# Moving the token normalisation of three cross attentions from VectorE to GpSimd

## The chip, the cores and the metric

The kernel runs on one core of a Trainium2 chip. The metric is the device time of one execution in microseconds (us). The engines have one instruction queue each and run side by side, tied by semaphores: TensorE (PE, matrix products), VectorE (DVE), ScalarE (ACT), GpSimd (POOL) and SyncE (SP, which issues transfers).

## The reference, cut to what matters

Sixteen sequences of 256 tokens, 128 wide, go through four layers of attention and feed-forward. Each attention takes the layer-normed tokens as queries and adds its result to the tokens. Three of the attentions, called `l0`, `l1c` and `l3` in the kernel, are cross attentions onto a context of 64 keys with 16 heads of 8, and each begins with the same norm:

```python
def _layernorm(x, axis=-1, eps=1e-05):
    m = jnp.mean(x, axis=axis, keepdims=True)
    v = jnp.var(x, axis=axis, keepdims=True)
    return (x - m) / jnp.sqrt(v + eps)

x = x + _L0_xattn_ref(_layernorm(x), ctx_512, ctx_512, ...)     # l0
x = x + _L1_xattn_ref(_layernorm(x), ctx_512, ...)              # l1s (self) and l1c (cross)
x = x + _L3_xattn_ref(_layernorm(x), ctx_512, ...)              # l3
```

## The kernel before

The tokens `x` stay in SBUF for the whole program as 32 tiles of 128 tokens, `[128, 32, 128]` in float32, two tiles for each of the 16 sequences. One function, `attention_rows`, builds five attentions. `units` (`U`) is the number of pieces into which the heads of one sequence are cut: `U` is 1 in `l0`, `l1c` and `l3`, where one step of the loop does one whole sequence, and 4 in the self attentions `l1s` and `a1`. The trace leaves digits at the end of a name out, so `l_xn` is the tile `xn` of `l0` (about 22 to 148 us of the span) and of `l3` (about 2296 to 2417 us); `l1c_xn` is that of `l1c` (about 741 to 869 us).

Each engine walks through the same steps j, in a software pipeline that `emit` writes out, and in step j works on different sequences. `at(k)` gives the sequence j + k. With one unit there are 4 steps of lead. In step j, in this order on each queue:

- DVE: `maxima` of sequence j+1, first half (L808); `ln_apply` of j+3 (L792, two instructions, one for each tile, that write `xn`); `ln_stats` of j+4 (L776 and L781: two bn_stats, two bn_aggr into `mv`); `residuals` of j-2 (L877); `maxima` of j+1, second half; then the end of sequence j-1: `turn_sums` (L817), `divide` (L822, L828) and `turn_back` (L838).
- POOL: `context` of j+2 (L967); `lay_values` of j+1 (L993), which first waits for `pv_done`, the value product of sequence j-1; `rstds` of j+4 (L931 and L933: variance plus epsilon, then the power -0.5); `preset` of j+1 where there is an output bias (L961, in `l0` and `l1c`); `keys` of j+2 (L978, two instructions).
- PE: `shift` of j (L533); `turn` of j+2 (L439: `xn` transposed, in both tiles); `scores` of j+1, first half (L485); `values` of j-1 (L566); `project_out` of j-2 (L608, L611); `scores` of j+1, second half; `scores_t` of j+1 (L500); `project_qk` of j+2 (L449, L451, L454), which waits for the residual of j-2, since both use the bank `psum_act`.
- ACT: the two exponentials of j (L668), `turned` of j+2 (L675), `copy_qk` of j+2 (L691, L694, L698), and in `l1c` one copy more (L729).

`turn` of j+2 waits for `proj_out` of j+1, that is for the last of the copies of ACT (L698) in the step before. There is one buffer `xn`, one `mv` and one `rstd`. `ln_apply` of sequence b therefore waits for `xn_turned` to reach b (the transpose of sequence b-1). The statistics of the next sequence come behind `ln_apply` on the same queue, so nothing need guard `mv`.

Of the kernel before, what the change touches and what calls it, by code (L numbers as in the profile page):

```python
# [12 lines left out]
ALU = mybir.AluOpType  # L13
AX = mybir.AxisListType

P = 128
NB = 16
T = 256
TT = T // P
# [16 lines left out]
def wait(eng, sem, value):  # L36

    if isinstance(value, int) and value <= 0:
        return
    eng.wait_ge(sem, value)  # L40
# [234 lines left out]
def attention_rows(nc, name, K, W, *, dh, units, x, out, after=None, norms=(), affine_q=None, affine_kv=None,  # L275
# [10 lines left out]
    U = units  # L286
# [19 lines left out]
    with ExitStack() as ctx:  # L306
        def sb(nm, shape, dt=F32):
            return ctx.enter_context(nc.sbuf_tensor(f"{name}_{nm}", shape, dt))

        def sem(nm):  # L310
            return nc.alloc_semaphore(f"{name}_{nm}")
# [13 lines left out]
        xn = sb("xn", [P, TT, P])  # L325
        mv = sb("mv", [P, NLN, TT, 2])
        st6 = sb("st6", [P, NLN, TT, 6])
        rstd = sb("rstd", [P, NLN, TT])
# [21 lines left out]
        if add_t is not None:  # L350
# [8 lines left out]
        xn_ready, xn_turned = sem("xn_ready"), sem("xn_turned")  # L359
        laid = sem("laid")  # L360
        st_step, stats, veps_ready, rstd_ready, scaled, gained, shifted = (
            [sem(f"{nm}{i}") for i in range(NLN)]
            for nm in ("st_step", "stats", "veps_ready", "rstd_ready", "scaled", "gained", "shifted"))
# [47 lines left out]
        def inside(n, limit=N):  # L411
            return not isinstance(n, int) or 0 <= n < limit

        block = ctx.enter_context(nc.Block())

        @block.sync
# [318 lines left out]
        def _(dve):  # L735
# [31 lines left out]
            def ln_stats(b, i):  # L767
                src = (x if i == 0 else residual)[:, bass.ds(b * TT, TT), :]
                if i > 0:
                    ready = shifted if norms[i - 1] is not None else scaled  # L770
                    dve.wait_ge(ready[i - 1], b + 1)
                elif merge:
                    dve.wait_ge(merged, 2 * TT * (b + 1))
                dve.sem_inc(K["passed"], 1)
                for t in range(TT):
                    last = dve.bn_stats(st6[:, i, t, :], src[:, t, :])  # L776
                last.then_inc(st_step[i], 1)
                dve.wait_ge(st_step[i], b + 1)
                dve.sem_inc(K["passed"], 1)
                for t in range(TT):  # L780
                    last = dve.bn_aggr(mv[:, i, t, :], st6[:, i, t, :])  # L781
                last.then_inc(stats[i], 1)

            def ln_apply(b, i):
                dve.wait_ge(rstd_ready[i], b + 1)
                src = (x if i == 0 else residual)[:, bass.ds(b * TT, TT), :]
                final = i == NLN - 1
                if final:
                    wait(dve, xn_turned, b)
                dst = xn if final else residual[:, bass.ds(b * TT, TT), :]  # L790
                for t in range(TT):
                    last = dve.tensor_scalar(dst[:, t, :], src[:, t, :], mv[:, i, t, 0:1], rstd[:, i, t:t + 1],  # L792
                                             ALU.subtract, ALU.mult)
                last.then_inc(xn_ready if final else scaled[i], 1)

            def maxima(n, pos, half):

                dve.wait_ge(s_ready, 2 * n + half + 1)
                if half == 0:
                    wait(dve, st_ready, 2 * (n - 1))  # L800
                src = psum_s[:, :, 0:SC].rearrange("p i (h k) -> p i h k", k=P if before else NK)
                dst = negm[:, pos % 2, :, 2 * half * CG:2 * (half + 1) * CG]
                if U == 1:
                    src = src.rearrange("p i (q s) k -> p q i s k", q=TT)
                    dst = dst.rearrange("p q (i s) -> p q i s", i=2)
                else:
                    dst = dst.rearrange("p q i -> p i q")
                dve.tensor_reduce(dst, src, AX.X, ALU.max, negate=True).then_inc(max_done, 1)  # L808
# [58 lines left out]
            def residuals(b):  # L867
                dve.wait_ge(w_done, b + 1)
                view = psum_act[:, 0:T].rearrange("p (t d) -> p t d", t=TT)
                dst = out[:, bass.ds(b * TT, TT), :]  # L870
                base = dst
                if bob is not None:
                    dve.wait_ge(preset_done, b + 1)
                else:
                    base = (residual if residual is not None else x)[:, bass.ds(b * TT, TT), :]
                dve.sem_inc(K["passed"], 1)
                dve.tensor_tensor(dst, view, base, ALU.add).then_inc(res_done, 1)  # L877

            def emit(at):
                n, b, u, pos = at(0)  # L880
                n1, b1, u1, _ = at(-1)
                nw, bw, uw, _ = at(-2)
                nn, bn, un, posn = at(1)
                if inside(nn):
                    maxima(nn, posn, 0)
                for when, what, i in sorted(plan, key=lambda p: (-p[0], p[2])):
                    na, ba, ua, posa = at(LEAD - when)
                    if inside(na) and ua == 0:
                        if what == "merge":
                            merge_choice(ba, (posa // U) % 2, i)  # L890
                        elif what != "gather":
                            ln_stats(ba, i) if what == "stats" else ln_apply(ba, i)
                residual_now = inside(nw) and uw == U - 1 and store_t is None
                if residual_now and inside(nn):
                    residuals(bw)
                if inside(nn):
                    maxima(nn, posn, 1)
                    if before:
                        join_maxima(nn, posn)
                if paired and U == 1 and inside(n1):  # L900
                    turn_sums(n1, n1)
                    divide(n1)
                    turn_back(n1, b1)
                if paired and U == 4:
                    n3, b3, u3, _ = at(-3)
                    if inside(n1) and u1 == U - 1:
                        turn_sums(b1, n1)
                    if inside(nw) and uw == U - 1:
                        divide(bw)
                    if inside(n3) and u3 == U - 1:  # L910
                        turn_back(b3, b3)
                if not paired and inside(n1):
                    if per_unit or U == 1:
                        normalise(n1, n1, b1, u1)
                    elif u1 == U - 1:
                        normalise(b1, n1, b1, u1)
                if residual_now and not inside(nn):
                    residuals(bw)
# [6 lines left out]
        def _(pool):  # L925
            pool.wait_ge(K["ahead"], W.count)

            def rstds(b, i):
                pool.wait_ge(stats[i], b + 1)
                pool.sem_inc(K["passed"], 1)  # L930
                pool.tensor_scalar(veps[:, i, :], mv[:, i, :, 1], EPS, None, ALU.add).then_inc(veps_ready[i], 1)  # L931
                pool.wait_ge(veps_ready[i], b + 1)
                pool.tensor_tensor(rstd[:, i, :], veps[:, i, :], K["half"][:, 0:TT], ALU.pow).then_inc(rstd_ready[i], 1)  # L933

            def gather(b, par, i):
                if i == 0:
# [79 lines left out]
            def emit(at):  # L1016
                n, b, u, pos = at(0)
                nn, bn, un, posn = at(1)
                n2, b2, u2, pos2 = at(2)
                if pm is not None and inside(n):  # L1020
                    mask(n, pos, 0)
                    mask(n, pos, 1)
                if U == 1 and inside(n2):
                    context(b2, pos2)
                if not per_unit and inside(nn) and un == 0:
                    lay_values(bn, posn)
                for when, what, i in sorted(plan, key=lambda p: (-p[0], p[2])):
                    na, ba, ua, posa = at(LEAD - when)
                    if inside(na) and ua == 0:
                        if what == "gather":  # L1030
                            gather(ba, (posa // U) % 2, i)
                        elif what == "stats":
                            rstds(ba, i)
                        elif what == "apply" and i < NLN - 1 and norms[i] is not None:
                            gain(ba, i)
                if bob is not None and inside(nn) and un == 0:
                    preset(bn)
                if not per_unit and inside(n2):
                    keys(n2, b2, u2, pos2)

            run(pool, emit)


# [2060 lines left out]
```

## Time and profile before

| | us |
|---|---|
| median of 3 runs | 2518.63 (2516.05 to 2523.42) |
| the profiled execution | 2544.34 |
| its span, first to last instruction | 2542.6 |

| engine | busy us | share of the span |
|---|---|---|
| PE | 2192.1 | 86% |
| DVE | 1813.8 | 71% |
| ACT | 1335.9 | 53% |
| POOL | 1245.5 | 49% |

The mean granted TensorE clock is 0.941 of full speed. The shares are means over some fifteen stages with different limits; the three stages that the change touches take about 126, 128 and 121 us of the span. A timeline row gives the start, the duration (of several instructions where xN is more than one), the engine, the line, and output<-inputs; in square brackets stands the idle time just before it and what ended it, where that was noted.

### The profile page before, as it was taken

The page shows a single profiled execution, that of the slowest core. Times are in us where ns is not written, and L with a number is a line of the kernel's source. Part 1 is how long each engine was busy: PE and PEld are TensorE (multiplying, and loading weights), DVE is VectorE, ACT ScalarE, POOL GpSimd, SP SyncE. Part 2 cuts the span into 40 slices and gives each one's busy share as a digit, 9 for nine tenths or more (in the row PEclk, how much of TensorE's full clock was granted, in tenths as well). Part 3 has the DMA queues.
Part 4 walks back from the last instruction along what each step waited for, and adds up shares of the span by engine and source line. Part 5 has one row for each costly group of instructions (what it writes and reads, how often), then busy time and mean ns, then how long its engine had stood idle before and what let it go on. Part 6 is the DMA issues. An engine that isn't in the chain of part 4 may idle for free. (4 is left out here: it accounts for less than half of the span.)

```text
span 2542.6 us, 67314 instructions
## 1 busy us (share of the span) xinstructions
PE 2192.1 (86%) x22345; PEld 1689.5 (66%) x22352; DVE 1813.8 (71%) x4650; ACT 1335.9 (53%) x2821; POOL 1245.5 (49%) x1940
## 2 busy tenths in 40 slices
PE   5878997999988768779999997899888999998855
PEld 4557995666656557657777776666667888885523
DVE  5975554666659754578888867677698866667977
ACT  2434552343434435535555556444476888883456
POOL 4546635555534357277777745333164333324333
PEclk9968998999999869989999998999989999999978
DMA  8022211000000213200000000000000312210000
GB/s 310 10 110 74 77 53 29 14 12 12 12 2 1 78 57 97 78 18 13 9 10 9 9 2 20 10 1 0 15 5 5 92 57 66 58 47 14 1 9 25
DMA packets 82031, 96.69 MB, mean 38 GB/s; under 512 B 16720, under 2 KB 61136, under 8 KB 79760
## 3 DMA queue, kind: packets, MB, share of 16 engines
q1 hardware_dynamic: 73616, 77.12, 9.6%
q0 software_dynamic: 8192, 16.79, 2.3%
q8 instruction: 115, 1.88, 0.3%
q14 instruction: 108, 0.88, 0.1%
HBM read 56.51 MB, written 37.36 MB: 37 GB/s over the span
## 5 line engine op out<-in xcount | busy, mean ns | idle before, releaser
L1722 DVE TENSOR_TENSOR l2f_h_lo<-l2f_h,l2f_h_hi 128x512 fp32r<-128x512 f32 x256 | 187.5, 764 | 100.8 <-ACT l2f_h_hi L1643 100.7
L1012 POOL TENSOR_TENSOR a_pm<-a_pt,tri_post 128x256 f32<-128x256 f32 x256 | 179.6, 730 | 87.2 <-ACT a_pt L668 86.7
L808 DVE TENSOR_REDUCE l1s_negm<-l1s_s 128x6 bf16<-128x768 f32 x128 | 123.1, 961 | 109.2 <-PE l1s_s L485 109.1
L1650 ACT ACTIVATE l2f_h<-l2f_f,ahead 128x512 f32<-128x512 f32 x256 | 174.3, 688 | 49.6 <-DVE l2f_h_lo L1722 32.5
L808 DVE TENSOR_REDUCE a_negm<-a_s 128x4 bf16<-128x1024 f32 x128 | 156.1, 1219 | 32.0 <-PE a_s L485 30.3
L668 ACT ACTIVATE l1s_pt<-l1s_st 128x768 f32<-128x768 f32 x128 | 96.9, 811 | 155.5 <-PE l1s_st L523 155.5
L1817 POOL TENSOR_TENSOR l2f_acc<-l2f_tmp,l2f_acc 128x512 f32<-128x512 f32 x56 | 73.0, 1303 | 207.2 <-DVE l2f_tmp L1740 207.2
L1643 ACT ACTIVATE l2f_h_hi<-l2f_h 128x512 fp32r<-128x512 f32 x256 | 154.5, 633 | 0.0
L668 ACT ACTIVATE a_pt<-a_st 128x1024 f32<-128x1024 f32 x128 | 126.5, 1065 | 3.3 <-PE a_st L523 3.3
L684 ACT ACTIVATE a_q_hi<-a_pa 128x256 fp32r<-128x256 f32 x64 | 24.5, 383 | 185.0 <-PE a_pa L451 185.0
L1534 PE MATMUL l2f_f<-l2f_x_hi,l2f_w_hi 128*128 128x512 f32 x256 | 101.9, 398 | 1.2 <-POOL l2f_w_lo L1804 1.2
L1536 PE MATMUL l2f_f<-l2f_x_lo,l2f_w_hi 128*128 128x512 f32 x256 | 100.5, 392 | 0.0
L1535 PE MATMUL l2f_f<-l2f_x_hi,l2f_w_lo 128*128 128x512 f32 x256 | 100.4, 392 | 0.0
L1534 PE MATMUL l2f_y<-l2f_h_hi,l2f_w_hi 128*128 128x512 f32 x256 | 100.4, 392 | 0.0
L1536 PE MATMUL l2f_y<-l2f_h_lo,l2f_w_hi 128*128 128x512 f32 x256 | 99.7, 390 | 0.0
L1535 PE MATMUL l2f_y<-l2f_h_hi,l2f_w_lo 128*128 128x512 f32 x256 | 99.6, 389 | 0.0
L808 DVE TENSOR_REDUCE l_negm<-l_s 128x16 bf16<-128x1024 f32 x64 | 77.5, 1210 | 21.1 <-PE l_s L485 20.0
L500 PE MATMUL a_st<-a_q_f,a_k_f 32*128 32x256 f32 x1024 | 86.3, 387 | 0.1
L2290 DVE SCALAR_TENSOR_TENSOR l0f_z<-l0f_bank_b,l0f_bt,l0f_a_s 128x128 f32<-128x128 f32 x144 | 43.9, 346 | 55.7 <-ACT l0f_a_s L2118 47.9
L943 POOL DMA_INDIRECT a_got<-expert_rows,a_slot x64 | 68.3, 1067 | 22.9 <-POOL a_slot L939 13.0
L2360 POOL DMA_INDIRECT expert_rows<-l1f_xn,l1f_slots x64 | 63.8, 997 | 27.9 <-DVE l1f_slots L2214 12.8
L2043 PE MATMUL l0f_bank_g<-l0f_z,l0f_w 128*128 128x128 f32 x576 | 76.1, 275 | 0.0
(575 smaller groups left out, 7076.4 us busy)
## 6 DMA issues: line engine op xcount, KB each, us to landing
expert_rows<-zeros SPq DMA_DIRECT2D x16, 1056.0 KB, 17.5
l2f_wrow<-weights_by_expert SPq DMA_DIRECT2D x64, 256.0 KB, 3.2
l0f_w<-in_l0f_w SPq DMA_DIRECT2D x8, 640.0 KB
l0f_x_in_sb<-expert_rows SPq DMA_DIRECT2D x72, 64.0 KB
expert_rows<-l0f_y SPq DMA_DIRECT2D x72, 64.0 KB, 1.6
l1f_x_in_sb<-expert_rows SPq DMA_DIRECT2D x72, 64.0 KB
expert_rows<-l1f_y SPq DMA_DIRECT2D x72, 64.0 KB
ahead<-in_l2f_w SPq DMA_DIRECT2D x6, 512.0 KB, 4.5
```

The source lines that it names most:

```text
L500: pe.matmul(psum_st[:, i, kt * T:kt * T + T - q0], kb_f[rows(i), par_k, kt * P:(kt + 1) * P], q_f[rows(i), par_q, q0:T], start=kt == 0, st ...
L668: act.activation(pt[:, pos % 2, 2 * g:2 * g + 2, :], psum_st[:, 2 * g:2 * g + 2, 0:SC], ACT.Exp, scale=scale).then_inc(exp_done, 1)
L808: dve.tensor_reduce(dst, src, AX.X, ALU.max, negate=True).then_inc(max_done, 1)
L1012: last = pool.tensor_tensor(pm[:, par, heads_, kt, :], pt[:, par, heads_, kt * (T + P):kt * (T + P) + P], K["tri_post"][:].unsqueeze(1).br ...
L1534: pe.matmul(dst, w_hi[:, wpar, cols], hi, start=start, stop=False)
L1535: pe.matmul(dst, w_lo[:, wpar, cols], hi, start=False, stop=False)
L1536: return pe.matmul(dst, w_hi[:, wpar, cols], lo, start=False, stop=stop)
L1643: act.activation(h_hi[:, pos % 2, j], h[:, j], ACT.Identity).then_inc(h_high, 1)
L1650: act.activation(h[:, j], psum_f[j][:], ACT.Gelu, bias=col(e, j)).then_inc(h_ready, 1)
L1722: dve.tensor_tensor(h_lo[:, pos % 2, j], h[:, j], h_hi[:, pos % 2, j].bitcast(F32), ALU.subtract)\
L1817: pool.tensor_tensor(acc[:, bass.ds(c * CH, CH)], tmp[:, pos % 2], acc[:, bass.ds(c * CH, CH)], ALU.add).then_inc(added, 1)
L2043: last = pe.matmul(bank_g[j % 2][:, g * P:(g + 1) * P], w2[:, j % 2, blk * P:(blk + 1) * P], z[:, j % 2, i, :], start=i == 0, stop=i == 1)
```

## The change

For one-unit attentions alone, the norm is taken from DVE's queue and given to POOL's. A new function `norm(b)` on POOL stands in the place of the step "apply" in the order of the plan: in step j, behind `lay_values` of j+1 and ahead of `rstds` of j+4. It waits for `rstd_ready` and for `xn_turned`, then subtracts the mean from both tiles in one 128x256 tensor_tensor, waits for that on a new semaphore `centred`, and multiplies both tiles by the reciprocal root in another, in place in `xn`. Mean and root are read with a step of zero along each row. `ln_stats` of b now first waits on DVE until `xn_ready` is b, that is until `norm` of b-1 is through with `mv`; in step j it is the statistics of j+4 that wait for `norm` of j+3, of the same step. Self attentions (`U` of 4) are as before.

```diff
+        centred = sem("centred")
         block = ctx.enter_context(nc.Block())
@@ ln_stats, on DVE
                 dve.sem_inc(K["passed"], 1)
+                if U == 1:
+                    wait(dve, xn_ready, b)
                 for t in range(TT):
                     last = dve.bn_stats(st6[:, i, t, :], src[:, t, :])
@@ emit, on DVE
-                        elif what != "gather":
-                            ln_stats(ba, i) if what == "stats" else ln_apply(ba, i)
+                        elif what == "stats":
+                            ln_stats(ba, i)
+                        elif what == "apply" and U == 4:
+                            ln_apply(ba, i)
@@ on POOL, behind rstds
+            def norm(b):
+                pool.wait_ge(rstd_ready[0], b + 1)
+                wait(pool, xn_turned, b)
+                src = x[:, bass.ds(b * TT, TT), :]
+                pool.sem_inc(K["passed"], 1)
+                o = [P, TT, P]
+                pool.tensor_tensor(xn[:], src, mv[:, 0, :, 0:1].broadcast_to(o), ALU.subtract).then_inc(centred, 1)
+                pool.wait_ge(centred, b + 1)
+                pool.tensor_tensor(xn[:], xn[:], rstd[:, 0, :].unsqueeze(2).broadcast_to(o), ALU.mult).then_inc(xn_ready, 1)
@@ emit, on POOL
                         elif what == "stats":
                             rstds(ba, i)
+                        elif what == "apply" and U == 1:
+                            norm(ba)
```

## Rows read from the trace of the kernel before

**Rows 1.** The page, busy time and share of each engine.
```profile
PE 2192.1 (86%) x22345; PEld 1689.5 (66%) x22352; DVE 1813.8 (71%) x4650; ACT 1335.9 (53%) x2821; POOL 1245.5 (49%) x1940
```

**Rows 2.** Busy time by window: length, PE, PEld, DVE, ACT, POOL, PEclk, DMA share, GB/s.
```profile
60.00:120.00 60.00, 51.50 (x719) 35.66 (x718) 55.65 (x123) 28.26 (x59) 29.55 (x61) 1.00 0.09 35
772.00:840.00 68.00, 58.69 (x813) 42.52 (x814) 62.37 (x130) 32.52 (x72) 33.27 (x66) 1.00 0.00 0
2327.00:2388.00 61.00, 53.68 (x760) 37.51 (x756) 56.34 (x127) 27.50 (x63) 26.39 (x54) 1.00 0.00 0
2480.00:2510.00 30.00, 17.54 (x104) 10.68 (x107) 26.43 (x92) 21.07 (x36) 11.80 (x26) 0.85 0.07 20
```

**Rows 3.** Timeline, DVE in one step of `l0`, maxima to maxima.
```profile
67.76 1.23 DVE L808 TENSOR_REDUCE l_negm<-l_s 128x16 bf16<-128x1024 f32 x1
68.90 0.72 DVE L792 TENSOR_SCALAR l_xn<-tokens_x,l_mv,l_rstd 128x128 f32 x2
69.55 0.47 DVE L776 BATCH_NORM_STATS2 l_st<-tokens_x 128x6 f32 x2
70.56 0.42 DVE L877 TENSOR_TENSOR tokens_x<-l_pa,tokens_x 128x256 f32 x1
70.90 1.21 DVE L808 TENSOR_REDUCE l_negm<-l_s 128x16 bf16<-128x1024 f32 x1
```

**Rows 4.** Timeline, `l0`, from one residual to POOL's next value layout.
```profile
63.54 0.42 DVE L877 TENSOR_TENSOR tokens_x<-l_pa,tokens_x 128x256 f32 x1
...
64.11 0.67 PE L449 MATMUL l_pa<-l_xq_t,ahead 128*128 128x256 f32 x2 [0.20 <-DVE tokens_x L877]
...
66.76 0.43 PE L439 MATMUL l_pa<-ident,l_xn 128*128 128x128 f32 x2 [0.53 <-ACT l_v_f L698]
...
67.55 1.07 PE L566 MATMUL l_nd<-l_pt,l_vb 128*32 128x256 f32 x16
...
68.83 0.46 POOL L993 TENSOR_TENSOR l_vb<-l_v_f,l_own_half 128x128 f32<-128x128 f32 x1 [1.49 <-issue]
```

**Rows 5.** Timeline, the same stretch in `l1c` and in `l3`.
```profile
801.89 0.42 DVE L877 TENSOR_TENSOR tokens_x<-l1c_pa,tokens_x 128x256 f32 x1 [0.15 <-issue]
...
802.82 0.70 PE L449 MATMUL l1c_pa<-l1c_xq_t,ahead 128*128 128x256 f32 x2
...
806.30 1.07 PE L566 MATMUL l1c_nd<-l1c_pt,l1c_vb 128*32 128x256 f32 x16
...
2333.97 0.42 DVE L877 TENSOR_TENSOR tokens_x<-l_pa,tokens_x 128x256 f32 x1
...
2337.71 1.07 PE L566 MATMUL l_nd<-l_pt,l_vb 128*32 128x256 f32 x16
```

**Rows 6.** Timeline, DVE residuals: the first or last of each run of equal steps.
```profile
119.36 0.42 DVE L877 TENSOR_TENSOR tokens_x<-l_pa,tokens_x 128x256 f32 x1
...
772.31 0.42 DVE L877 TENSOR_TENSOR tokens_x<-l1c_pa,tokens_x 128x256 f32 x1 [0.15 <-issue]
...
838.94 0.42 DVE L877 TENSOR_TENSOR tokens_x<-l1c_pa,tokens_x 128x256 f32 x1 [0.22 <-PE l1c_pa L611]
...
2327.30 0.42 DVE L877 TENSOR_TENSOR tokens_x<-l_pa,tokens_x 128x256 f32 x1
...
2388.26 0.42 DVE L877 TENSOR_TENSOR tokens_x<-l_pa,tokens_x 128x256 f32 x1
```

**Rows 7.** Groups of POOL by line and form, then timeline rows of dependent pairs.
```profile
L978 POOL TENSOR_TENSOR l_kb_hi<-l_k_f,own_slot 128x256 fp32r<-128x256 f32 x32 | 19.6, 612 | 32.9 <-ACT l_k_f L691 22.3 <-PE l_st L533 10.5
...
63.66 0.22 POOL L931 TENSOR_SCALAR l_veps<-l_mv 128x2 f32<-128x2 f32 x1 [1.32 <-DVE l_mv L781]
63.97 0.71 POOL L933 TENSOR_TENSOR l_rstd<-l_veps,half 128x2 f32<-128x2 f32 x1
...
1290.33 0.72 POOL L955 TENSOR_TENSOR l_base<-l_base,ahead 128x256 f32 x1 [0.19 <-POOL l_base L952]
```

**Rows 8.** Timeline, DVE in the lead-in of `l0`.
```profile
27.97 0.60 DVE L792 TENSOR_SCALAR l_xn<-tokens_x,l_mv,l_rstd 128x128 f32<-128x128 f32 x2 [1.25 <-POOL l_rstd L933]
```

## The prediction

> **What bounds the kernel now.** I read the page first: PE is the busiest engine and POOL is idle half the time [rows 1], so a move from DVE to POOL looks free. But these are averages over all stages, and the change touches three. The windows over the even part of each come next [rows 2]: in `l0` DVE is busy 55.65 of 60 us (93%), in `l1c` 62.37 of 68 and in `l3` 56.34 of 61 (92% in both), PE 51.50, 58.69 and 53.68 (86 to 88%), POOL under half. DVE is the fullest engine there, so work taken from it could count. Last I read the order of one step in the timeline. On DVE [rows 3] it is closed up: maxima until 68.99, the two instructions of the norm at 68.90, the statistics at 69.55, the residual from 70.56 to 70.98, the second maxima at 70.90.
>
> The other thing to read is the loop that runs through the other engines. I call the end of a residual R and the end of the value product V. In [rows 4] R is 63.54 + 0.42 = 63.96. The projection on PE was released by it (64.11), ScalarE copies its result, that releases the transpose (66.76), scores follow, and the value product ends at 67.55 + 1.07 = 68.62. So from R to V it is 4.66 us, and none of it can go earlier while R stands. The next residual ends at 70.98, V + 2.36. The sum is 7.02; over eight steps from 63.54 to 119.36 the step is 6.98 [rows 4, 6]. So two chains are tight at once: DVE's queue, and this loop, which DVE closes.
>
> **What the change removes.** Two tensor_scalar of DVE in each step. From the start of the first to the start of the statistics they hold the queue 69.55 - 68.90 = 0.65 us [rows 3]. By themselves they would give back up to 0.65 us a step.
>
> **What it adds.** Two GpSimd instructions of 128x256, the second waiting for the first. The nearest row is `l_kb_hi` in the same stages: 128x256, two inputs, one with a step of zero, 612 ns [rows 7]. The link between two dependent POOL instructions is 63.97 - 63.66 - 0.22 = 0.09 us where nothing stands between, and 0.19 in the `a1` stage, where an increment does [rows 7]; `norm` has none between. So the pair is 0.61 + 0.09 + 0.61 = 1.31 us. The bound above is the pair of 128x256 in `a1`: 0.72 + 0.19 + 0.72 = 1.63 [rows 7]. Below I know of no row under 0.61. I take 1.31, since shape, stage and the zero step are those of the change. The new semaphore and the register for the new wait I cost at nothing, hidden in DVE's idle time that follows.
>
> DVE works the norm out in one pass, POOL needs two. The Trainium skill speaks against the move: GPSIMD Engine Reference, "Engine selection", gives elementwise work to VectorE, with GpSimd about twice as slow where there are two inputs. Twice the 0.42 us of the 128x256 residual of DVE [rows 3] would be an estimate of 0.84 us for each instruction and 1.77 for the pair, and the time would be about 2571 us; the 612 ns of the row says that this is too dear for this shape.
>
> **Where it is put** decides. `norm` of j+3 stands behind `lay_values` of j+1, which waits for `pv_done` of sequence j-1, that is for V. In [rows 4] it starts at 68.83, V + 0.21, after 1.49 us of idle, and takes 0.46. Only then does `norm` begin, though its roots were ready a step ago and the transpose that frees `xn` was over at 67.19 [rows 4]. It ends at V + 0.21 + 0.46 + 1.31 = V + 1.98. Behind the new wait on DVE are queued the statistics of j+4, the residual of j-2, the second maxima, the end of sequence j-1: all of it. DVE had its first maxima done at 68.99 = V + 0.37 and is then idle for 1.7 us. With 0.07 for the handoff the statistics start at V + 2.05; from there to the residual's end it is 70.98 - 69.55 = 1.43 as now [rows 3]. So R comes at V + 3.48, where it was V + 2.36. And for R wait PE's projection (the bank) and, through it, the next transpose and the next V; for the second maxima waits PE's `shift`. Nothing in the loop gives the time back: it is new period = (R to V) + 3.48.
>
> - `l0`: 4.66 + 3.48 = 8.14 against 6.98: +1.16 us a step.
> - `l3`: R 2334.39, V 2338.78 [rows 5], so 4.39 + 3.48 = 7.87, against (2388.26 - 2327.30) / 9 = 6.77 [rows 6]: +1.10.
> - `l1c`: R 802.31, V 807.37 [rows 5], 5.06 apart, but the projection started only 0.51 behind R, since PE was still busy with the longer output projection; with R later it is free and starts 0.15 behind, as in `l0` [rows 4]. So 5.06 - 0.36 + 3.48 = 8.18, against (838.94 - 772.31) / 9 = 7.40 [rows 6]: +0.78.
>
> This holds in the steps with statistics on DVE and a value product for POOL to wait for: j from 1 to 11, 11 in each stage. 11 x (1.16 + 1.10 + 0.78) = 33.4 us.
>
> **The ends of each stage.** In the lead-in DVE waits for POOL's root and norms at once (27.97) [rows 8]; twice before the first scores the pair of 1.31 plus the copy of the context ahead of it stands in a chain where 0.5 to 0.65 stood, part of the first behind DVE's memsets: I estimate 1.5 us a stage, 4.5 in all, bounds 0 and 2.5 a stage. In the last steps (j of 12 and on) there are no statistics and so no wait; DVE saves one norm, and PE sets the pace there: -0.2 a stage at most. Other work of POOL moved past: `rstds`, `preset` and `keys` now follow the pair, but they wait for DVE's statistics and ScalarE's copy anyway, which come later by as much. No DMA is issued by any of it.
>
> **Sum.** 33.4 + 4.5 - 0.6 = +37.3 us. The profiled execution took 2544.34, so 2581.6 profiled; the median of plain runs lies 25.7 below the profiled one, and I put the same difference on it: 2518.63 + 37.3 = 2556 us, 1.5% slower.
>
> **The rivals.**
> - *Dear pair* (same mechanism): POOL at 0.72 and the link 0.19 add 0.32 x 33 = 10.6 us: 2567. For it: all 128x256 work of POOL in `a1` is at that price. Chance 0.16.
> - *The clock falls.* PE now waits some 1.3 us before each projection, and its busy share in `l0` falls from 86% to 51.5/60 x 6.98/8.14 = 74%. At 86 to 88% the granted clock was 1.00 (2.4 GHz) in all three [rows 2]; in the last stage, with PE busy 17.54 of 30 us, it was 0.85 [rows 2], so part of the time at 1.2 GHz. If a stage ran wholly at 1.2 GHz, the 3 us or so of PE work between R and V would double: +3 x 33 = 99 at most; a tenth to a half of that in 2566 to 2605. Against it: 74% is nearer to 86 than to 58. Chance 0.06.
> - *Partly covered*: something between R and V waited for DVE and not for R, so that V comes earlier behind R than now. In `l0` each link has R as its source, so I can't name it; half the cost would be 2537. Chance 0.08.
> - *The other side: POOL's pair is ready in time.* If `lay_values` did not hold POOL until V, `norm` could start at the transpose's end (67.19) and end at 68.50, before DVE's maxima (68.99). The point from which it decides is that: the pair must end by V + 0.37. Then DVE gives back 0.65 us a step, R comes at V + 1.71, and the loop is 6.37 in `l0`: -0.61 x 33 = -20, with the lead-in -16: 2503. For it: DVE is the fullest engine. Against it: POOL's idle 1.49 us before L993, ended 0.21 behind V, in every such step that I looked at. Chance 0.05.
> - *Both cancel*, within 0.3%: 0.03.
>
> The forecast itself, 2545 to 2562, has 0.62.
>
> **How the numbers follow.** 0.3% is 7.6 us, about what a measurement of this kernel can tell from no change. Faster is the other side alone, 0.05; the same 0.03; all else is slower, 0.92. The range must leave out no more than 0.2: from 2540, which leaves out the other side, the cancelling case and half of the partly covered one, to 2573, which takes in the dear pair and the light end of the clock.
>
> **What the profile after would show.** On DVE in the three stages the idle time in front of L776 goes from none to some 1.7 us a step, released by POOL's `xn`; POOL's two new rows of 0.6 to 0.7 us directly behind L993; residuals 8.1 us apart in `l0`, 8.2 in `l1c`, 7.9 in `l3`; DVE's busy share there down to about 73%; the granted clock still 1.00. I am wrong if L993 and the pair come before V, if the pair is under 0.5 us (then the first maxima cover more of it), or if residuals stand closer than 7 us.

## The result, and the profile after

| | before | changed |
|---|---|---|
| median of 4 runs, us | 2517.34 (2514.05 to 2523.42) | 2561.80 (2559.02 to 2564.26) |
| ratio, 95% interval | | 1.0165 (1.0153 to 1.0178) |
| span of the profiled execution | 2542.6 | 2562.3 |

The kernel is 44.5 us slower; 37.3 was the sum of the prediction. (The profiled execution of the kernel before came in slower than its plain runs; the section on the kernel before, again, says why.) The page of the changed kernel, busy time by engine, beside [rows 1]:

```profile
PE 2198.5 (86%) x22352; PEld 1692.9 (66%) x22352; DVE 1786.0 (70%) x4554; ACT 1337.5 (52%) x2821; POOL 1304.4 (51%) x2036
```

DVE has 96 instructions and 28 us of work fewer, POOL 96 instructions and 59 us more. That DVE does less says nothing of the time. The even stretch of each stage, `l0`, `l1c`, `l3`, as in [rows 2] (length, PE, PEld, DVE, ACT, POOL, clock, DMA share, GB/s):

```profile
60.00:135.00 75.00, 55.19 (x778) 38.50 (x776) 53.16 (x111) 29.84 (x63) 43.65 (x83) 1.00 0.07 28
790.00:863.00 73.00, 57.50 (x792) 41.58 (x792) 52.64 (x106) 32.57 (x72) 42.54 (x81) 1.00 0.00 0
2336.00:2406.00 70.00, 53.73 (x756) 37.58 (x756) 51.69 (x107) 27.50 (x63) 36.89 (x71) 1.00 0.00 0
```

No engine is full any more: DVE is at 71 to 74%, where it was at 92 to 93, and PE at 74 to 79%. Where every engine has gaps, a loop of waits must hold the stage. The timeline of one step of `l0` in the changed kernel, the counterpart of [rows 3, 4], shows it:

```profile
70.51 0.42 DVE L880 TENSOR_TENSOR tokens_x<-l_pa,tokens_x 128x256 f32 x1
...
71.08 0.67 PE L450 MATMUL l_pa<-l_xq_t,ahead 128*128 128x256 f32 x2 [1.36 <-DVE tokens_x L880]
...
74.53 1.07 PE L567 MATMUL l_nd<-l_pt,l_vb 128*32 128x256 f32 x16
74.74 1.23 DVE L811 TENSOR_REDUCE l_negm<-l_s 128x16 bf16<-128x1024 f32 x1
...
75.80 0.46 POOL L1008 TENSOR_TENSOR l_vb<-l_v_f,l_own_half 128x128 f32<-128x128 f32 x1 [1.49 <-issue]
...
76.22 0.61 POOL L946 TENSOR_TENSOR l_xn<-tokens_x,l_mv 128x256 f32<-128x256 f32 x1
...
76.91 0.61 POOL L948 TENSOR_TENSOR l_xn<-l_xn,l_rstd 128x256 f32<-128x256 f32 x1
...
77.68 0.49 DVE L779 BATCH_NORM_STATS2 l_st<-tokens_x 128x6 f32 x2 [1.71 <-POOL l_xn L948]
...
78.70 0.42 DVE L880 TENSOR_TENSOR tokens_x<-l_pa,tokens_x 128x256 f32 x1
```

Read it from R to R. R is 70.93; the projection waited 1.36 us for it; the value product ends at 75.60 (V, R + 4.67); the value layout on POOL follows 0.20 behind, the pair directly behind that, DVE's statistics behind the pair after 1.71 us of idle, and the next R is 79.12, V + 3.52. The view by the tile `xn` counts it: who waited for it, in `l0` and `l3`, and then in `l1c`:

```profile
L946 POOL TENSOR_TENSOR l_xn<-tokens_x,l_mv x32: 612/614/622, 25.1 to 2411.6; 128x256 f32<-128x256 f32 x32
L948 POOL TENSOR_TENSOR l_xn<-l_xn,l_rstd x32: 613/614/615, 25.8 to 2412.3; 128x256 f32<-128x256 f32 x32
  DVE l_st L779: 46.9, 29
...
  DVE l1c_st L779: 23.8, 14
```

70.7 us of DVE waiting, in 43 waits. Its counterpart of [rows 6], the first and the last residual of the nine even steps:

```profile
62.39 0.42 DVE L880 TENSOR_TENSOR tokens_x<-l_pa,tokens_x 128x256 f32 x1 [0.15 <-issue]
...
135.66 0.43 DVE L880 TENSOR_TENSOR tokens_x<-l_pa,tokens_x 128x256 f32 x1
...
790.03 0.42 DVE L880 TENSOR_TENSOR tokens_x<-l1c_pa,tokens_x 128x256 f32 x1
...
863.33 0.42 DVE L880 TENSOR_TENSOR tokens_x<-l1c_pa,tokens_x 128x256 f32 x1
...
2335.63 0.42 DVE L880 TENSOR_TENSOR tokens_x<-l_pa,tokens_x 128x256 f32 x1
...
2406.22 0.42 DVE L880 TENSOR_TENSOR tokens_x<-l_pa,tokens_x 128x256 f32 x1
```

Where the time went, from the residuals and the first statistics of each stage and the first instruction of the next (us; difference to the first profile of the kernel before):

| | `l0` | `l1c` | `l3` | sum |
|---|---|---|---|---|
| one even step, mean of nine, before / changed | 6.97 / 8.14 | 7.40 / 8.14 | 6.77 / 7.84 | |
| nine even steps | +10.5 | +6.7 | +9.6 | +26.8 |
| first statistics to first residual (lead-in) | +5.7 | +6.2 | +7.3 | +19.3 |
| last even residual to the next stage | +0.5 | -0.5 | +0.4 | +0.4 |
| stage | +16.7 | +12.4 | +17.4 | +46.5 |

The sum stands against 44.5 between the medians, so the three changed stages account for all of it.

### The profile page after: what moved, and what is told of

It is laid out like the page before. It is cut to its first block and busy times, and to the rows that moved or that the text cites. A ratio compares the mean times of both kernels' runs of the same rounds, so it can differ in the third digit from the quotient of the medians.

```text
span 2562.3 us, 67324 instructions
## 1 busy us (share of the span) xinstructions
PE 2198.5 (86%) x22352; PEld 1692.9 (66%) x22352; DVE 1786.0 (70%) x4554; ACT 1337.5 (52%) x2821; POOL 1304.4 (51%) x2036
```

## Experiments

Theory: the pair costs because GpSimd begins it only behind the value product and VectorE stands still for it, and all that VectorE does behind the wait is in the loop. Rivals: GpSimd's instructions are too slow wherever they stand; the late `xn` holds the transposes; another stage took the time. All ratios are to the kernel before on the same chip; a first group of four ran on one chip (before: 2520.75 us), a second (2540.87) and a third (2546.47) later on another. Ratios are compared within a group or between groups, times only within a group. In the second and third group the intervals reach up to 0.3% or 7.6 us to either side.

### The norm ahead of the value layout

```diff
+                na, ba, ua, posa = at(LEAD - 1)
+                if U == 1 and inside(na):
+                    norm(ba)
                 if not per_unit and inside(nn) and un == 0:
                     lay_values(bn, posn)
...
-                        elif what == "apply" and U == 1:
-                            norm(ba)
```

> The changed kernel with norm of j+3 put ahead of lay_values of j+1 on GpSimd's queue, nothing else. Theory (the pair costs because it begins only behind the value product V and VectorE waits for it): it now begins at the transpose's end and is over before VectorE's first maxima; the idle time in front of the statistics goes from 1.7 to about 0, residuals stand about 6.4 us apart in l0, 6.3 in l3 and, since PE's own loop sets it there, 7.4 in l1c. Against 8.14, 7.84 and 8.14 of the changed kernel that is 11 x 4.0 = 44 us: about 2518, the time of the kernel before within 8, since the longer lead-in stays. Rival (GpSimd's two instructions are themselves too slow, wherever they stand): steps stay above 7.5 us in l0 and the time above 2540.

Measured: 2522.25 us, ratio 1.0008 (0.9998 to 1.0018). One step of `l0`:

```profile
74.72 0.43 PE L440 MATMUL l_pa<-ident,l_xn 128*128 128x128 f32 x2 [0.53 <-ACT l_v_f L699]
...
75.41 0.61 POOL L946 TENSOR_TENSOR l_xn<-tokens_x,l_mv 128x256 f32<-128x256 f32 x1
...
75.51 1.07 PE L567 MATMUL l_nd<-l_pt,l_vb 128*32 128x256 f32 x16
75.62 1.22 DVE L811 TENSOR_REDUCE l_negm<-l_s 128x16 bf16<-128x1024 f32 x1
76.11 0.61 POOL L948 TENSOR_TENSOR l_xn<-l_xn,l_rstd 128x256 f32<-128x256 f32 x1
...
76.87 0.49 DVE L779 BATCH_NORM_STATS2 l_st<-tokens_x 128x6 f32 x2
```

The pair is the same two times 0.61 us, but it begins 0.26 behind the transpose and is over at 76.72, under the first maxima (to 76.84); no wait is left. Moving two instructions past one other took 1.6% off. With the pair no faster than before, the loss is gone: its place decides whether its 1.3 us are paid. The steps are 6.70, 7.41 and 6.45 us: `l1c` as expected, the other two 0.3 and 0.15 above it.

### Two buffers of mv

```diff
-        mv = sb("mv", [P, NLN, TT, 2])
+        mv = sb("mv", [P, 2 if U == 1 else NLN, TT, 2])
...
                 if U == 1:
-                    wait(dve, xn_ready, b)
+                    wait(dve, stats[0], b)
+                    wait(dve, xn_ready, b - 1)
```

(with bn_aggr, the roots and the subtraction taking the buffer of the sequence's parity)

> The changed kernel with two buffers of mv in the one-unit attentions, so that the statistics of b wait for norm of b-2 and not of b-1; norm stays behind lay_values. Theory (it is VectorE's wait that closes the loop, not the late xn): VectorE no longer waits, steps of about 6.4, 6.3 and 7.4 us as with norm ahead, though xn is finished as late as in the changed kernel; 2505 to 2520. Rival (the late xn holds the transposes): steps stay near 8 us, and 2550 or more.

Measured: 2512.45 us, ratio 0.9967 (0.9954 to 0.9981), the fastest form that computes everything and is clear of the kernel before. In its profile the three stages are 4.6 us shorter than in the first profile of the kernel before, near the low end of that interval. GpSimd still begins behind V (in the rows below at 74.81, V + 0.62, as in the changed kernel), so `xn` is as late as there, and the steps are 6.69, 7.41 and 6.44 us. So the late `xn` holds nobody: the transpose wants it only in the next step. It was the guard of `mv`, one buffer, that made VectorE wait. The steps are those of the experiment above to 0.01 us, which says that something else now sets them. The 9.8 us between the medians of the two lie mostly in the lead-ins, 103.5 us with the norm ahead and 96.0 with two buffers. DVE lost 0.65 us a step and only 0.28 came back in `l0`. The timeline of one step with two buffers in `l0`:

```profile
69.64 0.70 PE L450 MATMUL l_pa<-l_xq_t,ahead 128*128 128x256 f32 x2
...
72.33 0.44 PE L440 MATMUL l_pa<-ident,l_xn 128*128 128x128 f32 x2 [0.53 <-ACT l_v_f L699]
...
73.12 1.07 PE L567 MATMUL l_nd<-l_pt,l_vb 128*32 128x256 f32 x16
...
74.44 0.68 PE L612 MATMUL l_pa<-ahead,l_o_t 128*128 128x128 f32 x4 [0.25 <-ACT l_xq_t L676]
...
74.81 0.61 POOL L948 TENSOR_TENSOR l_xn<-tokens_x,l_mv 128x256 f32<-128x256 f32 x1
...
75.39 1.04 PE L501 MATMUL l_st<-l_q_f,l_kb_f 32*128 32x256 f32 x14
75.41 0.42 DVE L881 TENSOR_TENSOR tokens_x<-l_pa,tokens_x 128x256 f32 x1 [0.16 <-issue]
...
76.35 0.70 PE L450 MATMUL l_pa<-l_xq_t,ahead 128*128 128x256 f32 x2
```

The residual is over at 75.83, but the projection starts at 76.35 with no idle time before it: PE was busy with the value scores until 76.43. From projection to projection it is 6.71 us: PE's own products, and the idle time in which it waits for the copies of ScalarE (0.53) and for the copy of the transpose (0.25). That loop is next. How near it was could be seen in the kernel before: in [rows 4] PE is idle for only 0.20 us before the projection, waiting for the residual, and over `l0` these waits are 0.19 to 0.27 us. Only by about as much could an earlier residual help, and 0.28 came back.

### VectorE's wait between bn_stats and bn_aggr

```diff
                 if U == 1:
-                    wait(dve, xn_ready, b)
+                    wait(dve, stats[0], b)
                 for t in range(TT):
                     last = dve.bn_stats(st6[:, i, t, :], src[:, t, :])
...
                 dve.wait_ge(st_step[i], b + 1)
+                if U == 1:
+                    wait(dve, xn_ready, b)
```

> The changed kernel with VectorE's wait for xn_ready put between bn_stats and bn_aggr (only mv needs guarding; st6 is guarded by the statistics before). Theory: every link behind the wait stands in the loop, so the 0.62 us from the first bn_stats to the first bn_aggr, now done during the wait, shorten each step by as much: 7.5, 7.2 and 7.5 us, 33 steps x 0.62 = 20 us less, about 2541. Rival (something else, such as the projection or ScalarE, is next close behind): less than 8 us come back.

Measured: 2539.40 us, ratio 1.0079 (1.0061 to 1.0097): 1.0165 - 1.0079 is 0.86%, 22 us less than the changed kernel; steps 7.49, 7.49 and 7.19.

```profile
78.29 0.47 DVE L779 BATCH_NORM_STATS2 l_st<-tokens_x 128x6 f32 x2
80.17 0.25 DVE L786 BATCH_NORM_AGGREGATE l_mv<-l_st 128x2 f32<-128x6 f32 x2 [1.40 <-POOL l_xn L950]
```

The bn_stats are done in what was idle time and each step is shorter by 0.65 in all three stages: the links behind the wait stand in the loop one for one.

### Half of the pair

```diff
-                pool.tensor_tensor(xn[:], src, mv[:, 0, :, 0:1].broadcast_to(o), ALU.subtract).then_inc(centred, 1)
-                pool.wait_ge(centred, b + 1)
-                pool.tensor_tensor(xn[:], xn[:], rstd[:, 0, :].unsqueeze(2).broadcast_to(o), ALU.mult).then_inc(xn_ready, 1)
+                pool.tensor_tensor(xn[:], src, mv[:, 0, :, 0:1].broadcast_to(o), ALU.subtract).then_inc(xn_ready, 1)
```

> The changed kernel without the multiplication by the reciprocal root in the one-unit attentions (left out of the computation): norm is one GpSimd instruction. Theory: the pair stands wholly in the loop; without its second half, 0.69 us from start to start, the steps are 7.45, 7.15 and 7.45 us, 33 x 0.69 = 23 us less, and 3 to 6 less in the lead-ins: 2533 to 2537. Rival (GpSimd's instructions are partly covered): under 12 us less.

Measured (the multiplication is left out, so `xn` is only centred and the result is not that of the reference): 2529.86 us, ratio 1.0056 (1.0033 to 1.0078), 1.09% or 27 us below the changed kernel, where 26 to 29 were expected; steps 7.45, 7.46 and 7.15, the expected ones to 0.01. A GpSimd instruction of this pair costs its whole 0.69 us in each step.

### The first three norms on VectorE

```diff
+        def early(b):
+            return isinstance(b, int) and b < 3
...
-                        elif what == "apply" and U == 4:
+                        elif what == "apply" and (U == 4 or early(ba)):
                             ln_apply(ba, i)
...
-                        elif what == "apply" and U == 1:
+                        elif what == "apply" and U == 1 and not early(ba):
                             norm(ba)
```

(with the first four statistics on VectorE no longer waiting for `xn_ready`, and `centred` counted from the fourth norm)

> The changed kernel with the norms of the first three sequences of each one-unit attention back on VectorE (steps -3 to -1); from the fourth on GpSimd does them. The even steps must stay at 8.1, 8.1 and 7.8 us. In the profiles the way from the first statistics to the first residual is 39.6, 36.9 and 38.6 us in the changed kernel and 33.8, 30.7 and 31.3 before. Theory (the lead-ins lost some 13 us of the 46, through the pair in their chain and through the clock that fell behind it): these come back nearly whole, 9 to 13 us: about 2550. Rival (the lead-in cost is only the 1.5 us a stage of the prediction, the rest is in the first even steps): 3 to 5 us come back, about 2558.

Measured: 2574.76 us, ratio 1.0121 (1.0092 to 1.0150). The changed kernel has 1.0165 in its first measurement and 1.0157 on this chip (below), so 0.36 to 0.44% or 9 to 11 us came back; the intervals are too wide to part the two expectations. In the profile the lead-ins are 36.7, 35.8 and 35.4 us: 7.2 of the 19.3 came back, not 9 to 13. Up to the first maxima the pair is out of the chain, but the clock was low in this execution too. Three windows of 7 us from the start of `l3`, first the kernel before, then this one:

```profile
2296.00:2303.00 7.00, 5.87 (x55) 5.39 (x56) 4.37 (x24) 1.33 (x5) 2.54 (x7) 0.76 0.38 122
2303.00:2310.00 7.00, 5.11 (x42) 3.64 (x39) 3.48 (x8) 0.38 (x1) 3.29 (x7) 0.76 0.01 2
2310.00:2317.00 7.00, 5.01 (x79) 3.79 (x80) 3.48 (x8) 4.75 (x10) 2.78 (x7) 1.00 0.00 0
```

```profile
2318.70:2325.70 7.00, 6.46 (x47) 5.82 (x48) 4.38 (x24) 0.39 (x1) 2.55 (x7) 0.50 0.34 122
2325.70:2332.70 7.00, 5.49 (x47) 4.29 (x46) 3.48 (x8) 1.33 (x5) 3.30 (x7) 0.74 0.01 2
2332.70:2339.70 7.00, 5.63 (x61) 4.11 (x61) 2.97 (x6) 4.44 (x8) 4.01 (x8) 0.74 0.00 1
```

In the first window DVE does the same 24 instructions in both, and the clock is 0.76 in one and 0.50 in the other.

### More keep-awake matmuls

```diff
-                        keep_awake(pe, K, psum_st[:, 0, :], 8)
+                        keep_awake(pe, K, psum_st[:, 0, :], 20)
...
-                    keep_awake(pe, K, psum_st[:, 0, :], 8 if U == 1 or per_unit else 24)
+                    keep_awake(pe, K, psum_st[:, 0, :], 20 if U == 1 else 8 if per_unit else 24)
```

> The changed kernel with 20 instead of 8 keep-awake matmuls at the two places of the lead-in of one-unit attentions. In the changed kernel the granted clock of l3 is 0.74, 0.74, 0.74 and 0.59 in the four windows of 7 us up to 2325, where before it is back at 1.00 in the third. Theory (half or more of the lead-in loss is the clock): the clock of these windows rises to 0.9 or more, and 3 to 8 us come back: 2554 to 2559. Rival (the loss is the wait itself, and the clock only follows): the clock may rise, the time stays at 2560 to 2564 or grows by the added matmuls.

Measured: 2581.65 us, ratio 1.0156 (1.0127 to 1.0186). The interval holds the changed kernel's 1.0165 and the 1.0157 of its repetition as well as the 3 us less of the theory, so the time decides nothing. In the profile the lead-ins are 35.0, 35.0 and 36.1 us, 9.0 less than in the changed kernel's first profile and 5.4 less than in its repetition. The four windows of `l3` have 0.74, 0.80, 0.93 and 0.83, so the clock did not rise to the 0.9 that the theory asked for. Inconclusive.

### Two buffers and the first three norms on VectorE

(both edits together)

> Two buffers of mv and the first three norms on VectorE together: GpSimd norms, VectorE never waits for them in the even steps, and the lead-in is that of the kernel before. Theory: even steps of 6.7, 7.4 and 6.4 us as with two buffers alone, and what of the lead-in is still longer than before comes back (one stage at most 2 to 3 us): 2505 to 2512, 0.4 to 0.6% faster than the kernel before. Rival (the two buffers have already taken the lead-in back): 2512, as without it.

Measured: 2538.14 us, ratio 0.9985 (0.9972 to 0.9997). The steps are 6.70, 7.41 and 6.46, but nothing came on top of two buffers alone (0.9967, 0.9954 to 0.9981); the intervals overlap. Two buffers had already taken the lead-in back: there it is 32.6, 33.0 and 30.4 us, 96.0 in all, against 95.7 in the kernel before.

### The kernel before, again

> The kernel before once more, unchanged, for a second profile of it. In the first, the stage of routed experts between 872 and 1083 us took 211 us, against 190 in the profile of the changed kernel, which leaves it alone. Theory (the 25.7 us between the profiled execution and the median are a disturbance of that one stage): here the stage takes 190 to 195 us, the profiled execution 2515 to 2525, and the three one-unit stages the same as in the first profile within 0.5 us. Rival (the profile itself costs 25 us): about 2544 again.

Measured: 2542.56 us, ratio 0.9995 (0.9980 to 1.0010). The theory fell in its first half. From the start of the routed experts of layer 1 (872.2) to the first statistics behind them (1086.2) it was 214.0 us in the first profile; here it is 213.9, in the changed kernel's profile 193.2, in the four of the first group 192 to 195, and in all eight of the second and third group, which share a chip, 212.6 to 214.8. So this untouched stage goes with the chip and not with the kernel. Nor does the profiling cost the time: here the profiled execution took 2542.15 us against a median of 2542.56. The 25.7 us of the prediction are then most likely another chip, one on which this stage takes some 20 us more; on which chip the first profile was taken is not on record. The even steps of the three changed stages are the same on both: 6.97, 7.40 and 6.77, as in the first profile.

### The changed kernel, again, and both lead-in edits together

> The changed kernel once more, unchanged, as the anchor for the next two on the same chip. The two profiles of the kernel before show that the stage between 872 and 1083 us takes 211 us on some chips and 190 on others. Expected: even steps again 8.14, 8.14 and 7.84 us; from the first statistics to the first residual 39.5, 36.9 and 38.6 us within 1.5 if the clock falls the same way in each execution, further off if the granted clock of the lead-ins differs from run to run; ratio to the kernel before 1.015 to 1.018.

Measured: 2588.81 us, ratio 1.0157 (1.0132 to 1.0183). Even steps 8.14, 8.15 and 7.84; the lead-ins 37.8, 36.9 and 36.7 us, 1.7 and 1.9 shorter than in the first profile in `l0` and `l3`. In these two the clock differed as well: in `l0`, in the three windows of 7 us from 29.8 on, it was 0.76, 0.50 and 0.52 in the first profile and 1.00, 1.00 and 0.76 here. In `l1c`, where the windows have 0.73 to 0.78 in both, the lead-in is the same to 0.03 us. Set against the repetition of the kernel before, on the same chip, the three stages are 43.6 us longer, and the medians of this group are 42.3 apart.

> The changed kernel with the first three norms on VectorE and with 20 keep-awake matmuls in the lead-in. The three parts of the lead-in's loss are, from the profiles, 6.5 us up to the first maxima (the pair in the chain), 5.9 us that are even steps already, and 6.9 us left. Theory (what is left is TensorE at the lower clock): with the pair gone and the clock at 0.9 or more in the windows of l3, 10 to 13 us come back against the changed kernel on the same chip. Rival (the clock costs nothing on the path): 6 to 7 us, those of the pair alone.

Measured: 2577.98 us, ratio 1.0114 (1.0085 to 1.0143), 10.8 us below the changed kernel on the same chip. That is in the range of the theory, but the interval of 0.3% takes in the rival's 6 to 7 us too, and with the norms alone the ratio was 1.0121, so that the keep-awake matmuls are not shown to have added anything. The lead-ins are 33.3, 32.2 and 33.5 us, 12.4 less. The clock of `l3` was not at 0.9 throughout. Three windows of `l3` of this kernel, and after them the changed kernel on the same chip:

```profile
2313.90:2320.90 7.00, 6.46 (x66) 6.05 (x67) 4.37 (x24) 1.33 (x5) 2.54 (x7) 0.76 0.40 124
2320.90:2327.90 7.00, 5.68 (x88) 4.45 (x87) 3.48 (x8) 1.85 (x6) 4.49 (x10) 1.00 0.00 0
2327.90:2334.90 7.00, 5.03 (x43) 3.70 (x44) 3.07 (x6) 3.23 (x6) 2.79 (x7) 0.76 0.01 4
```

```profile
2325.20:2332.20 7.00, 5.60 (x47) 5.01 (x48) 2.73 (x16) 0.44 (x2) 3.75 (x8) 0.74 0.37 123
2332.20:2339.20 7.00, 4.23 (x36) 3.29 (x37) 2.63 (x10) 1.28 (x5) 4.80 (x10) 0.50 0.01 4
2339.20:2346.20 7.00, 5.64 (x62) 3.86 (x54) 2.67 (x5) 3.68 (x7) 3.97 (x8) 0.78 0.00 0
```

### Two buffers and more keep-awake matmuls

> Two buffers of mv and 20 keep-awake matmuls: whether the clock in the lead-in gives something on top of the best kernel so far (0.9967 of the kernel before). With two buffers alone the clock in l3 was 0.76, 0.76 and then 1.00. Theory (clock on the path): 2 to 5 us more, ratio 0.995 to 0.996. Rival (the lead-in waits for GpSimd and VectorE, not for TensorE): ratio 0.996 to 0.998.

Measured: 2540.41 us, ratio 0.9970 (0.9956 to 0.9984): nothing on top of two buffers (0.9967), as the rival had it. The lead-ins sum to 94.1 us, 1.9 less, which is within what they vary by.

### Does GpSimd hinder VectorE's multiplications?

```diff
                 for dst, ready in ((kb_hi, kb_hi_ready), (kb_f, kb_f_ready)):
-                    if U == 1:
+                    if U == 1 and dst is kb_f:
+                        pool.memset(dst[:, pos % 2, :], 0.0).then_inc(ready, 1)
+                    elif U == 1:
```

> Two buffers of mv, and the second of the two key instructions of GpSimd (kb_f) replaced by a memset of the same tile, which writes but reads nothing (so the keys of the value scores are left out of the computation). Taking 0.65 us of work from VectorE gave back only 0.29 a step in l0 (6.98 to 6.69), while the two multiplications of L828 grew from 0.94 to 1.3 us beside GpSimd's key instructions; without GpSimd beside them they take 0.49. Theory (VectorE's multiplications with two inputs from SBUF and GpSimd's instructions hinder each other): the pair of multiplications falls to 0.8 to 1.0 us, and steps of 6.3 to 6.45 us in l0 and 6.1 to 6.25 in l3; 5 to 9 us less than with two buffers alone. Rival (the length of these rows only mirrors another wait): steps of 6.7 and 6.4 as before.

Measured (the keys of the value scores are left out, so the result is not that of the reference): 2537.14 us, ratio 0.9953 (0.9936 to 0.9969), which the interval doesn't part from 0.9967. The multiplications of the two kernels in the even part of `l0`, first with two buffers alone, then with the memset (the timeline's rows of DVE and POOL around them):

```profile
71.38 0.61 POOL L995 TENSOR_TENSOR l_kb_hi<-l_k_f,own_slot 128x256 fp32r<-128x256 f32 x1 [0.38 <-ACT l_k_f L692]
...
71.49 1.27 DVE L832 TENSOR_TENSOR l_on_t<-l_nd_t,l_rec_nd 128x128 f32<-128x128 f32 x2
...
71.95 0.66 POOL L995 TENSOR_TENSOR l_kb_f<-l_k_f,own_slot 128x256 f32<-128x256 f32 x1
```

```profile
74.42 0.61 POOL L997 TENSOR_TENSOR l_kb_hi<-l_k_f,own_slot 128x256 fp32r<-128x256 f32 x1 [0.37 <-ACT l_k_f L692]
...
74.46 0.92 DVE L832 TENSOR_TENSOR l_on_t<-l_nd_t,l_rec_nd 128x128 f32<-128x128 f32 x2
...
74.98 0.31 POOL L994 MEMSET l_kb_f<- 128x256 f32 x1
```

At the end of `l0` in the kernel before, where no instruction of GpSimd runs beside them, they take:

```profile
140.69 0.49 DVE L828 TENSOR_TENSOR l_on_t<-l_nd_t,l_rec_nd 128x128 f32<-128x128 f32 x2 [0.15 <-DVE l_rec_nd L822]
```

The theory's first half holds: where the second GpSimd instruction beside them only writes, the two fall from 1.27 to 0.92 us. Its second half falls: the steps stay at 6.70 and 6.44 us, and at 7.41 in `l1c`. With 0.4 us less work on DVE no step got shorter, so DVE did not set them; what is left is PE's loop in the rows of the second experiment.

## Why the prediction was right

**What bounds the kernel.** Right in the main: DVE's queue and the loop that it closes. Where I wrote that the two instructions "would give back up to 0.65 us a step", the next limit, PE's loop, was missing.

**The price of the pair.** Right: 0.61 + 0.61, with 0.69 from start to start, in all 48 calls of `norm`; the dear pair of `a1` did not show. The Trainium skill's rule of about twice VectorE's time (GPSIMD Engine Reference, "Engine selection") would have made each instruction 0.84 us by the estimate of the prediction; the trace has 0.614 for this shape, so the measurement decides. The one-pass kernel shows that the price stands wholly in the loop.

**The place.** Right: L1008 behind V after 1.49 us of idle, the pair behind it, DVE idle 1.71 (1.7 forecast), R at V + 3.52 (3.48). The handoff to DVE was put at 0.07 us, for which no row was given; from the end of the pair (77.52) to the statistics (77.68) it is 0.16. The steps were forecast at 8.14, 8.18 and 7.87 and are 8.14, 8.14 and 7.84. Norm ahead and two buffers each take the wait away by another road and take the whole 1.6 to 2.0% with it, so it is shown and not only argued.

**The lead-in** is the term that was mis-sized: 4.5 us forecast, with a bound of 7.5. In the table it is 19.3, of which 5.9 are two steps that the forecast counted among its 11 (2 x (1.16 + 0.74 + 1.07)). 13.4 are left in this execution. In its repetition it is 15.7 - 5.9 = 9.8, or 11.1 against the repetition of the kernel before: over the bound each time. To the first maxima it is 2.1, 1.9 and 2.6 us, 6.5 in all, where I had 4.5. That is the pair: with the first norms on VectorE 5.4 of it came back. The rest, 3 to 7 us, has no term in the prediction. Part of it goes with the clock: in `l3` of the first profile the granted clock stood at 0.59 in the fourth window, where the kernel before has 1.00 again. PE's rows there:

```profile
2319.94 1.22 PE L450 MATMUL l_pa<-l_xq_t,ahead 128*128 128x256 f32 x2
...
2321.94 1.92 PE L534 MATMUL l_st<-ident_bf,l_negm 128*64 128x128 bf16 x32
```

The same groups take 0.67 and 1.08 us in the even part, at 1.00. But in `l0` at least it is the small part: in the repetition it had 1.00, 1.00 and 0.76 in its three windows, the repetition of the kernel before 0.81, 0.74 and 0.96, and the lead-in was still 5.4 us longer, of which 2.3 are the two steps and 2.2 the pair. How the rest divides between clock and wait stays open, since the lead-ins vary by up to 2 us a stage without any edit and no time of an experiment on the clock stood clear of the noise. In the even part the clock stayed at 1.00 with PE at 74 to 79%, so the rival of the falling clock did not come where I placed it; in the lead-ins it fell in one execution and not in the next.

**Sum and offset.** 33.4 + 4.5 - 0.6 against 32.7 (26.8 + 5.9), 9.8 to 13.4 and +0.4. The steps were right within 1 us; the error of the sum, 7 us, is the lead-in's and the end's (the last steps, forecast at -0.6). The range, drawn for a dear pair, had the room for it, and that part of its holding is luck. The 25.7 us between profile and median were put down to the profiling; they were most likely the chip's. As the same was put on both sides, it did no harm.

**The other side** did not come, but its two forms were built, and its price was wrong: forecast 6.37 us a step in `l0` and 16 us less than the kernel before, measured 6.70 and 6.69, and 1.5 us more (ratio 1.0008) and 8 us less (0.9967). The failed step is "the loop is 6.37": R to V of 4.66 holds only while the projection waits for R. With R earlier PE is still busy with the value scores. For `l1c` I had read this ("PE was still busy"), and yet the 0.61 us were counted over all 33 steps, its eleven too, where nothing came back (7.41 against 7.40). For `l0` and `l3` the idle time of PE before the projection, 0.20 us in [rows 4], was there to be read.

## What to carry to other kernels

A norm, or any step, is not moved to an engine but to a place in its queue: what stands ahead of it there, and what that waits for, is added to it, and everything behind a wait on it moves too. Where the new owner reads something of which there is one buffer (here 16 bytes of `mv` in each partition), the guard on the old owner's queue can be the cost; here a second buffer took all of it away and made the change a gain of 0.33%. Before promising what a relieved engine gives back, look at how long the next engine waits for it in each step: here PE waited 0.19 to 0.27 us in `l0`, and 0.28 us came back of 0.65. And measure profile against profile in the stages that were changed: one stage that nobody touched differed by 20 us from chip to chip.

## What the runs showed of the hardware

- The granted clock of a stage's lead-in differs between executions of one kernel: 0.76, 0.50 and 0.52 against 1.00, 1.00 and 0.76 in the same three windows of `l0` of the changed kernel, with lead-ins of 39.6 and 37.8 us. Where it didn't differ (`l1c`), the lead-ins were the same to 0.03 us.
- One stage that no edit touched took 192 to 195 us in the four profiles of one chip and 212.6 to 214.8 in the eight of another.
- Two DVE multiplications of 128x128, both inputs in SBUF, took 0.49 us in all with POOL idle, 0.94 in the kernel before, where they overlap mainly one GpSimd instruction that reads SBUF, 0.84 to 0.92 where the second GpSimd instruction is a memset, and 1.26 to 1.34 beside two reading ones in a row. The Trainium skill tells of a lock on a port that VectorE and GpSimd share, taken by a VectorE instruction with two SBUF inputs only against a GpSimd instruction that reads SBUF, and held for the whole instruction (SBUF — State Buffer, "SBUF: two separate sides"). The memset, which reads nothing, agrees with the first; that the lock is held for a whole instruction these rows don't show.
